# The q, k, v products of a token tile in two halves of 432 columns instead of three parts of 288

## The reference

```python
mod = silu(c) @ w_mod + b_mod                 # six vectors of 288 for each sequence
xn  = ln(x) * (1 + sc_msa) + sh_msa
q, k, v = split(xn @ w_qkv + b_qkv)           # 288 -> 3 * 288
q, k = ln(q), ln(k)                           # by head; blocks 0 and 2, not block 1
o   = softmax(q @ k.T / sqrt(18)) @ v
x   = x + g_msa * (o @ w_proj + b_proj)
xn2 = ln(x) * (1 + sc_mlp) + sh_mlp
x   = x + g_mlp * (gelu(xn2 @ w1 + b1) @ w2 + b2)   # 288 -> 1152 -> 288
```

## Time and profile before

| | us |
|---|---|
| time, median of 3 runs | 4935.15 (4934.62 to 4951.71) |
| the profiled execution: span from its first to its last instruction | 4936.2 |
| PE busy | 4437.6 (90%) |
| PEld busy | 3707.8 (75%) |
| DVE busy | 3672.0 (74%) |
| ACT busy | 2292.4 (46%) |
| POOL busy | 1147.6 (23%) |
| layers 0 and 1, one full slot, layer 0 | 42.52 |
| layer 2, one full slot | 48.13 |

### The profile page before, as it was taken

How to read it: one execution, slowest core, us unless ns; L and a number is a source line. 1 busy time by engine, 2 the same in 40 slices (tenths; PEclk the granted TensorE clock), 3 DMA queues, 4 the chain that set the end, 5 groups by cost and what they waited for, 6 DMA issues and landing times. The chain is left out here.

```text
span 4936.2 us, 125360 instructions
## 1 busy us (share of the span) xinstructions
PE 4437.6 (90%) x46073; PEld 3707.8 (75%) x46073; DVE 3672.0 (74%) x7659; ACT 2292.4 (46%) x3894; POOL 1147.6 (23%) x2045
## 2 busy tenths in 40 slices
PE   6754999999999996999999999967999999999998
PEld 4543788888888874888888888855777777777776
DVE  5665788888888864777666666757888888888885
ACT  1213555555555543444555544434545455554543
POOL 1002222222222221222222222222222222222221
PEclk9976899999999997999999999987999999999999
DMA  3001100100001011011101100011000001010100
GB/s 74 20 0 53 29 25 29 29 28 26 29 29 28 24 36 49 24 29 29 29 25 29 29 29 23 26 47 33 24 25 24 28 21 28 21 29 19 29 19 24
DMA packets 122230, 141.59 MB, mean 29 GB/s; under 512 B 14446, under 2 KB 117780, under 8 KB 122112
## 3 DMA queue, kind: packets, MB, share of 16 engines
q1 hardware_dynamic: 121968, 139.75, 10.3%
q10 hardware_dynamic: 144, 0.22, 0.0%
HBM read 110.87 MB, written 29.06 MB: 28 GB/s over the span
## 5 line engine op out<-in xcount | busy, mean ns | idle before, releaser
L869 DVE TENSOR_REDUCE mx<-S 128x4 f32<-128x1024 f32 x768 | 920.9, 1217 | 105.9 <-PE S L1111 102.8
L627 ACT ACTIVATE pT<-S 128x1024 f32<-128x1024 f32 x768 | 745.4, 1022 | 365.3 <-PE S L1139 361.2
L575 ACT ACTIVATE hf<-M 128x512 f32<-128x512 f32 (+1 forms) x480 | 266.7, 556 | 1042.5 <-PE M L1191 523.3
L504 POOL TENSOR_SCALAR hh<-hf 128x512 fp32r<-128x512 f32 (+1 forms) x480 | 277.9, 579 | 1218.4 <-ACT hf L575 1172.8
L1139 PE MATMUL S<-qT,kT 32*128 32x256 f32 x9216 | 427.4, 296 | 64.7 <-ACT pT L627 63.3
L1152 PE MATMUL A<-pT,V 128*32 128x256 f32 x6144 | 414.2, 387 | 26.1 <-ACT pT L627 26.1
L1139 PEld LDWEIGHTS S<-qT,kT 32*128 32x128 f32 x9216 | 330.7, 185 | 136.9 <-ACT pT L627 92.9
L1111 PE MATMUL S<-kT,qT 32*128 32x256 f32 x3072 | 361.3, 335 | 49.2 <-DVE mx L869 43.2
L1191 PE MATMUL M<-xh,w_hi 128*128 128x256 f32 x1728 | 382.8, 303 | 3.5 <-POOL xh L480 3.5
L1230 PE MATMUL M<-w_lo,hh 128*128 128x288 f32 x1728 | 361.2, 311 | 0.0
L928 DVE TENSOR_TENSOR xbo<-M,gM 128x288 f32<-128x288 f32 x192 | 87.1, 454 | 365.3 <-PE M L1230 353.6
(11 more groups left out here) (231 smaller groups left out, 10131.4 us busy)
## 6 DMA issues: line engine op xcount, KB each, us to landing
mid<-xbo SPq DMA_DIRECT2D x64, 288.0 KB, 3.2
xld<-mid SPq DMA_DIRECT2D x64, 288.0 KB, 3.2
xa<-mid SPq DMA_DIRECT2D x64, 288.0 KB, 3.6
gA<-gates SPq DMA_DIRECT2D x96, 144.0 KB, 3.4
gM<-gates SPq DMA_DIRECT2D x96, 144.0 KB, 3.0
xld<-in_x_dram SPq DMA_DIRECT2D x32, 288.0 KB, 3.6
xa<-in_x_dram SPq DMA_DIRECT2D x32, 288.0 KB, 3.5
out_dram<-xbo SPq DMA_DIRECT2D x32, 288.0 KB, 2.2
```

The lines of the kernel that those rows point to most:

```text
L504: pool.tensor_scalar(hh[:, 2 * f:2 * f + m, :].rearrange("p m c -> p (m c)"), hf[:, f % 2, 0:m * T], 1.0, 0.0, ALU.mult, ALU.add).then_inc ...
L575: act.activation(hf[:, f % 2, 0:c], MBANK[f % 2][:, 0:c], ACT.Gelu if rot else ACT.Gelu_apprx_tanh).then_inc(s["m_hf"], 1)
L627: act.activation(pT[:, g % 2, 2 * h:2 * h + 2, :], S[:, 2 * h:2 * h + 2, :], ACT.Exp, scale=float(HD) ** -0.5).then_inc(s["a_ex"], 1)
L869: dve.tensor_reduce(mx[:, p, :, :], S[:, r:r + 2, :].rearrange("p a (t k) -> p a t k", t=NT), AX.X, ALU.max).then_inc(s["a_mx"], 1)
```

## The change

The q, k and v weights are taken as one block of 864 columns and cut in two halves of 432 (`HALF`): half 0 is q and the first eight heads of k, half 1 the other eight heads of k and v. There are four products a sequence instead of six, 28 matmuls instead of 42. ACT copies each half out: in layers 0 and 2 in one instruction, into one buffer `qkv` of which `qk` and `vraw` are now views; in layer 1 in two instructions (q and half of k, or half of k and v). Waits for all parts now count to 4. On PE the parts are spread anew over the stretch, and `A_square`, which needs q and k of both tiles, comes behind the last half.

```diff
-    a_x=16, ..., a_qkv=6, a_qkvd=6,
+    a_x=16, ..., a_qkv=4, a_qkvd=4,
...
-        qk = sb("qk", [P, NT, 2 * D])
-        vraw = sb("vraw", [P, NT, D])
+        qkv = sb("qkv", [P, NT, 3 * D])
+        qk = qkv[:, :, 0:2 * D]
+        vraw = qkv[:, :, 2 * D:3 * D]
...
-                        wait(pool, "a_qkvd", n, 6)
+                        wait(pool, "a_qkvd", n, 4)
...
-                        if f == 4:
+                        if f == 1:
                             wait(act, "a_v", n, 0)
                         wait(act, "a_qkv", n, f + 1)
-                        i, part = (f // 2, f % 2) if f < 4 else (f - 4, 2)
-                        of = ABANK[f % 2][:, 0:D]
...
+                        i, part = f // 2, f % 2
+                        of = ABANK[part][:, 0:HALF]
+                        if eps is not None:
+                            op = act.activation(qkv[:, i, part * HALF:(part + 1) * HALF], of, ACT.Identity)
+                        elif part == 0:
+                            act.activation(qs[:, i, :, 0:HD], of[:, 0:D].rearrange("p (h d) -> p h d", h=H), ACT.Identity)
+                            op = act.activation(ks[:, i, 0:H // 2, 0:HD], of[:, D:HALF].rearrange("p (h d) -> p h d", h=H // 2), ACT.Identity)
                         else:
-                            to = (qs, ks)[part][:, i, :, 0:HD]
-                            of = of.rearrange("p (h d) -> p h d", h=H)
-                        act.activation(to, of, ACT.Identity).then_inc(s["a_qkvd"], 1)
+                            act.activation(ks[:, i, H // 2:H, 0:HD], of[:, 0:HALF - D].rearrange("p (h d) -> p h d", h=H // 2), ACT.Identity)
+                            op = act.activation(vraw[:, i, :], of[:, HALF - D:HALF], ACT.Identity)
+                        op.then_inc(s["a_qkvd"], 1)
...
                         if nxt is not None:
                             A_qkv(nxt, 2)
+                        if p is not None:
+                            A_shift(p)
+                        if nxt is not None:
                             A_qkv(nxt, 3)
                             if eps is not None:
                                 A_square(nxt)
-                            A_qkv(nxt, 4)
-                        if p is not None:
-                            A_shift(p)
-                        if nxt is not None:
-                            A_qkv(nxt, 5)
...
-                        tokens(ABANK[f % 2][:, 0:D], (xh, xl, xm), wqkv, i, slice(part * D, (part + 1) * D)).then_inc(s["a_qkv"], 1)
+                        i, part = f // 2, f % 2
+                        tokens(ABANK[part][:, 0:HALF], (xh, xl, xm), wqkv, i, slice(part * HALF, (part + 1) * HALF)).then_inc(s["a_qkv"], 1)
...
                         qkv(0)
                         if turns:
                             R_turn(d, 1, m)
+                        down0(0, 8)
+                        if turns:
+                            R_z(d)
+                        score(6)
                         qkv(1)
                         if turns:
-                            R_z(d)
-                        down0(0, 8)
-                        score(6)
-                        if turns:
                             R_y(d)
-                        qkv(2)
                         score(7)
-                        qkv(3)
                         down0(8, 16)
                         if turns:
                             R_out(d, p)
-                        qkv(4)
+                        qkv(2)
                         if p is not None:
                             A_turn_max(p)
                         down0(16, 27)
-                        qkv(5)
+                        qkv(3)
```

More of the change, by code:

```diff
@@ L30 @@
 NT = T // P
+HALF = 3 * D // 2
 KC, KP = 3, 96
@@ L46 @@
 PER_RUN = dict(
-    a_x=16, a_g=16, a_st=1, a_ve=1, a_rs=1, a_xn=2, a_xT=2, a_xf=3, a_xh=2, a_xl=1, a_qkv=6, a_qkvd=6,
+    a_x=16, a_g=16, a_st=1, a_ve=1, a_rs=1, a_xn=2, a_xT=2, a_xf=3, a_xh=2, a_xl=1, a_qkv=4, a_qkvd=4,
     a_sq=1, a_hs=1, a_nrm=1, a_v=2, a_T=4, a_qhi=2, a_khi=2, a_qlo=2, a_klo=2, a_S=12, a_mx=8,
@@ L583, in A_qkv @@
                                 wait(act, "a_nrm", qk_run(n), 0)
-                        if f == 4:
+                        if f == 1:
                             wait(act, "a_v", n, 0)
                         wait(act, "a_qkv", n, f + 1)
-                        i, part = (f // 2, f % 2) if f < 4 else (f - 4, 2)
-                        of = ABANK[f % 2][:, 0:D]
[L589 to L592, removed]
-                        else:
-                            to = (qs, ks)[part][:, i, :, 0:HD]
-                            of = of.rearrange("p (h d) -> p h d", h=H)
-                        act.activation(to, of, ACT.Identity).then_inc(s["a_qkvd"], 1)
+                        i, part = f // 2, f % 2
[5 more added lines that the diff above has]
+                            op = act.activation(ks[:, i, 0:H // 2, 0:HD], of[:, D:HALF].rearrange("p (h d) -> p h d", h=H // 2), ACT.Identity)
+                        else:
+                            act.activation(ks[:, i, H // 2:H, 0:HD], of[:, 0:HALF - D].rearrange("p (h d) -> p h d", h=H // 2), ACT.Identity)
+                            op = act.activation(vraw[:, i, :], of[:, HALF - D:HALF], ACT.Identity)
+                        op.then_inc(s["a_qkvd"], 1)
                     def A_square(n):
@@ L601, in A_square @@
                         wait(act, "a_hs", qk_run(n), 0)
-                        act.activation(sq, qk[:, :, :].rearrange("p t c -> p (t c)"), ACT.Square).then_inc(s["a_sq"], 1)
+                        act.activation(sq.rearrange("p (t c) -> p t c", t=NT), qk, ACT.Square).then_inc(s["a_sq"], 1)
                     def A_hi(n, f):
@@ L802, in M_xl @@
                         low_x(xf2, xh2[:, :, :], xl2[:, :, :], xm2).then_inc(s["m_xl"], 1)
-                    heads = qk[:, :, :].rearrange("p t c -> p (t c)").rearrange("p (g d) -> p g d", d=HD)
                     def A_heads_sum(n):
@@ L1148, in A_pv @@
                             if p is not None:
-                                wait(pe, "a_qkvd", p, 6)
+                                wait(pe, "a_qkvd", p, 4)
                         for i in range(NT):
```

## The result

| | before | after |
|---|---|---|
| median of 8 runs each, same chip | 4938.12 us (4929.43 to 4951.71) | 4957.07 us (4952.76 to 4973.03) |
| ratio | | 1.004 [1.0028, 1.0052] |
| profiled execution: its span | 4936.2 us | 4959.7 us |
| a second session, median | 4943.6 us (23 runs) | 4954.35 us (12 runs), ratio 1.0026 [1.0016, 1.0036] |

What follows compares the result with a forecast made beforehand. PE (90% busy) was taken as the bound, with DVE's maxima pacing layers 0 and 1 up to `score(6)` and its head norm layer 2; 32.5 - 9.9 - 9.9 + 4.2 - 17.6 = -0.7 us gave 4935 us, range 4905 to 4964.

Steps and rivals of the forecast that it cites:

- The products after `score(6)`: Layers 0 and 1, PE: three halves replace four parts and a wait of 0.66 goes, 0.34 us less a slot.
- rival 5: Matmuls of 432 columns cost in proportion or worse, so halves gain only the missing wait: 4950 us, chance 0.07.
- The copy of 432 columns: ACT: 0.53 us for a copy of 432 columns, between 0.41 for 288 and 0.598 for 512.
- The square: Layer 0: its later place delays DVE's chain and PE's turn of normed x, 1.16 us a slot, 32.5 in all.
- Rival 3: Layer 0: the square's delay doesn't reach PE, 4902 us, chance 0.11.
- The wait at `score(6)`: Layers 0 and 1: PE arrives earlier and waits 1.1 us for the same DVE maximum.
- Layer 2: Full slot 48.6 us, counted as 0.15 over the mean of 48.45, 4.2 us for 28 slots.
- Rival 4: Layer 2 is hit harder, by the full 0.84 us over its mean: 20 us more, 4954 us, chance 0.09.
- the wait before the down product: Layer 2: PE idles 1.04 us for the last gelu before the down product's first piece.
- The falls of the clock: Layers 0 and 1: counted as gone with one wait instead of two, 12 x 1.47 = 17.6 us saved.
- Rivals 1 and 2: Clock falls: 1, they stay, 4953 us, chance 0.17; 2, more frequent in layer 0, 4963 us, chance 0.11.
- the sum: All three layers: 32.5 - 9.9 - 9.9 + 4.2 - 17.6 = -0.7 us against the profiled execution.

Runs made afterwards that it cites:

- E3: Kernel before with only `A_square` moved, behind the last part instead of behind part 3: 4968.46 us, ratio 1.0063.
- E4: Kernel before, three parts of 288 columns, with part 1 behind `score(6)` and the down product's first piece ahead of `R_z`: 5007.19 us, ratio 1.0133.
- E12: Kernel after with four of the eight matmuls ahead of `score(6)` moved behind it in layers 0 and 1: 5026.56 us, one run.
- E10: Kernel after, unchanged, run again for a second profile: 4954.35 us, ratio 1.0026.
- E9: Kernel after with `R_z` ahead of the down product's first piece only in layer 2 slots without `nxt`: 4951.46 us, ratio 1.0014.
- E1: Kernel after with half 1 and `R_z` ahead of the down product's first piece in layer 2 alone: 4919.74 us, ratio 0.9955.
- E11: Kernel before, unchanged, run once again for a second profile: 4950.83 us.
- E2: Kernel after with DVE's `M_x2(d, 0)` ahead of the head sum in layers 0 and 1: 4932.81 us, ratio 0.9989.
- E7: E1 and E2 together, plus the square cut in two instructions, one for each tile: 4845.51 us, ratio 0.9796.
- E6: E1 and E2 together, plus half 1 ahead of `score(6)` and down product pieces moved earlier in layers 0 and 1: 4824.37 us, ratio 0.9755.

## Why the prediction was wrong, by its own steps

*What held.* The products after `score(6)`: layer 1's slot is 42.18, forecast 42.2. A matmul of 432 columns takes 0.196 (seven of them from 897.73 to 899.10), between my 0.194 and the proportional 0.201; rival 5 fell. The Trainium skill (TensorE: Matmul & The Clock Gate, Back-to-back issue gap) would have 0.1825 for it by its formula for the gap at the full clock, so here the measurement decides, as it did for 288 columns. The copy of 432 columns takes 0.53 as taken. The square: head sum at 1.87 (forecast 1.91), PE at the turn at 6.77 (6.78), slot 43.34 (43.3); E3 shows that the square makes this cost by itself. Rival 3 fell. The wait at `score(6)` is 0.97 (1.1). Layer 2: slot 48.60 (48.6), the DMA no longer binding. Rival 4 fell. That 48.60 is met exactly is in part luck: the wait before the down product is 0.78 and not 1.04, but from the turn of q and k to the slot's end it is 32.59 against 31.85, so of the 0.40 that shorter products and fewer group starts were to save, 0.04 came.

*Right for a wrong reason.* The falls of the clock went: at 1.00 in all full slots, no slot 1.5 longer. My reason was that one wait stands where two stood. E4 has one wait (1.40) and 14 falls in these layers; E12 has halves and one wait (1.51) and falls. What goes with the falls, in layers 0 and 1, is how long PE stands still in that stretch: 0.47 + 0.66 = 1.13 in two pieces, 1.40 and 1.51 bring them; 0.97 didn't in any of the seven profiles that have it. Rivals 1 and 2 fell. I had called the new wait as long as the old ones; it was 0.16 shorter.

*The step that failed: the sum.* For the stretches of 24 full slots it forecast +10.9, -17.0 and +3.6; the profiles show +10.6, -17.2 and +3.7. But it multiplied by 28 or 29 slots and left out all others. The slots that fill and empty the layers have the same moves and other waits. The fill of layer 2 went from 184.3 and 185.9 us (two profiles of before) to 193.8, 192.0 and 191.8 (after, E10, E9): +7.4. E1 takes about 5 of that back, so it is mostly the order of half 1, `R_z` and the down product; E3 puts 4.3 on the square alone, the two overlapping. A part of both goes through the clock: it was at its lower level for 30.7 us of this fill in both profiles of before, and for 44.4, 33.6 and 37.5 in those three. At the 1.47 us that 3.4 us cost in the earlier trace rows the difference of 7.8 is some 3 us, an estimate. From point 28 of layer 2 to its last it is about +2 (E1 takes that back too), from layer 1's last point to layer 2's first about +2.3 (E1 doesn't). Together 12 us that the sum had at nothing, against a measured +11 in the second session and +19 in the first; some 7 us of the first remain open. The kernel before varies by 31 us itself (4928 to 4959), and its two profiles, with 12 and 14 falls in full slots, differ by 13 us, so a part of that may be in what it was compared with; this is argued, not shown. In the one pair of profiles taken anew (E10, E11) the spans are even alike, 4948.8 and 4949.1, with the fill still +6.1.

*Luck.* 4957 lies inside the range, and near the 4953 and 4954 of rivals 1 and 4, but what those rivals say didn't happen, and none of the slower cases was about the slots that fill and empty the layers.

*What the forecast missed as a lesson.* It named both costs, the square and the place of `R_z`, and priced their effect on a full slot right, yet treated them as parts of the change. E1 and E2 show that neither was: 47.57 and 42.43 a slot with the halves kept.

## What to carry to other kernels

A per-slot sum can be exact and still give the wrong sign: work out the first and the last slots of each layer as well, above all where the gain and the loss in the full slots nearly cancel. When the edit of one engine's order moves a producer later, look at what stands behind its consumer in that queue, and move the urgent item ahead (E2), or cut the late work so that only its last piece is late (E7). A wait of the busiest engine for another engine's result is only a bound if nothing that could run stands behind it (E6).

## What the runs showed of the hardware

- The clock fell to its lower level (0.50 of full speed, mostly for some 3.4 us, at 1.5 us of time each) in full slots of layers 0 and 1 where PE had stood still for 1.13 to 1.51 us in the stretch around `score(6)` (in E4 and E12 the record of the fall begins 0.5 to 1.9 us after the wait's end): of 56 such slots in 12 and 14 (before, E11), 16 (E3), 14 (E4) and 22 (E12). So most slots with such a wait don't fall. With 0.97 as the longest wait it never did in full slots, in seven profiles. The Trainium skill (TensorE: Matmul & The Clock Gate, A second HAM failure mode) describes such falling back and forth from small gaps; these runs agree that it exists, and E4 and E12 add that lengthening one gap is enough to bring it back.
- The length that a wait must have isn't the same everywhere. Layer 2 has no fall in its full slots though PE waits there up to 1.65 us for `ks` before and 1.22 for `hf` in every slot of E4; only after the two waits of 2.38 and 2.32 for `ks` in E4 did it fall. What sets the two stretches apart wasn't tried.
- The last stretch of one and the same code took 91.6 and 81.6 us with 27 and 7 us at the lower clock. A profile pair alone would have put 10 us on the change.
- A square of 576 elements takes 0.69 us where that of 1152 takes 1.17, so cutting it in two costs ACT 0.2, and took 1.27 off layer 2's slot.
